# Another placement of the small pieces over the 44 iterations of a batch, and fewer filler matmuls in the last two units

## What is computed

```python
x = x + _L0_xattn_ref(_layernorm(x), ctx_512, ...)      # q,k,v and qc,kc,vc projections, two softmaxes, @ Wp
x = x + _L0_ffn_ref(_layernorm(x), ...)                 # gate, top-k tokens of each expert, two matmuls
# inside the first:
att = jnp.where(causal, einsum('bhqd,bhkd->bhqk', q, k) * scale, -inf)
y = einsum('bhqk,bhkd->bhqd', softmax(att), v) + einsum('bhqk,bhkd->bhqd', softmax(attc), vc)
```

## Time and profile before

| | |
|---|---|
| time, median of 3 runs | 1595.7 us (1590.92 to 1598.44) |
| the profiled execution: its time, its span | 1597.86 us, 1596.1 us |
| mean granted TensorE clock | 0.965 |
| busy in the span: PE, DVE, ACT, POOL | 95%, 70%, 57%, 34% |
| first exponential of batch 0, of batch 1, of batch 7; end of the last | 68.4, 216.9, 1111.3, 1249.8 us |

### The profile page before, as it was taken

How to read it: one execution, slowest core, us unless ns; L and a number is a source line. 1 busy time by engine, 2 the same in 40 slices (tenths; PEclk the granted TensorE clock), 3 DMA queues, 4 the chain that set the end, 5 groups by cost and what they waited for, 6 DMA issues and landing times. The chain is left out here.

```text
span 1596.1 us, 26481 instructions
## 1 busy us (share of the span) xinstructions
PE 1514.2 (95%) x9025; PEld 733.7 (46%) x9025; DVE 1123.7 (70%) x3056; ACT 910.7 (57%) x1754; POOL 546.1 (34%) x1009
## 2 busy tenths in 40 slices
PE   8899999999999999999999999999999868999997
PEld 4433444444444444444444444444443424666664
DVE  6878887887787788778877877788781274554441
ACT  2167777677766777677777677777767301112111
POOL 4122333442343225233433442451121302443342
PEclk9599999999999999999999999999999877999999
DMA  6776662855376556737672855377300211343432
GB/s 136 155 135 104 127 88 77 121 105 106 104 104 136 87 101 124 123 84 109 120 122 83 115 105 105 94 102 141 42 3 3 87 38 38 101 108 100 123 90 50
DMA packets 82490, 155.46 MB, mean 97 GB/s; under 512 B 13012, under 2 KB 46420, under 8 KB 82356
## 3 DMA queue, kind: packets, MB, share of 16 engines
q1 hardware_dynamic: 76212, 145.25, 47.0%
q0 software_dynamic: 6144, 8.52, 3.1%
HBM read 96.52 MB, written 53.08 MB: 94 GB/s over the span
## 5 line engine op out<-in xcount | busy, mean ns | idle before, releaser
L829 ACT ACTIVATE probs<-bank_ps 128x512 f32<-128x512 f32 (+1 forms) x1408 | 730.1, 579 | 247.9 <-PE bank_ps L613 239.0
L920 DVE TENSOR_REDUCE chunk_max<-bank_ps 128x1 f32<-128x512 f32 x1024 | 653.5, 683 | 144.0 <-PE bank_ps L652 140.2
L652 PE MATMUL bank_ps<-k_stack,q_stack 62*128 62x512 f32 (+3 forms) x1536 | 536.3, 432 | 7.4 <-DVE chunk_max L920 4.1
L613 PE MATMUL bank_ps<-q_stack,k_stack 64*128 64x512 f32 (+3 forms) x1536 | 512.8, 423 | 25.7 <-ACT probs L829 22.1
L652 PEld LDWEIGHTS bank_ps<-k_stack,q_stack 62*128 62x128 f32 x1536 | 248.2, 191 | 372.4 <-DVE chunk_max L920 202.2
L923 DVE CUSTOM_DVE_ANT_0 masked<-bank_ps,causal 128x128 bf16<-128x128 f32 (+3 forms) x512 | 232.9, 485 | 62.4 <-PE bank_ps L652 58.8
L631 PE MATMUL out_ps<-probs,v_cross 128*32 128x512 f32 x2048 | 275.7, 610 | 0.0
L613 PEld LDWEIGHTS bank_ps<-q_stack,k_stack 64*128 64x128 f32 x1536 | 234.5, 189 | 83.2 <-ACT probs L829 76.3
L1093 POOL TENSOR_TENSOR pool_idle<-pool_idle 128x1 f32<-128x1 f32 x292 | 56.4, 193 | 582.5 <-ACT probs L829 386.1
L1406 ACT ACTIVATE h<-h_ps,b1T 128x512 f32<-128x512 f32 x64 | 44.0, 687 | 254.5 <-PE h_ps L1352 220.4
L1352 PE MATMUL h_ps<-ff_yT,w1T 128*128 128x512 f32 x256 | 122.6, 615 | 1.0 <-DVE ff_yT L1419 1.0
(11 more groups left out here) (165 smaller groups left out, 1384.0 us busy)
## 6 DMA issues: line engine op xcount, KB each, us to landing
parts_dram<-parts SPq DMA_DIRECT2D x70, 512.0 KB, 2.7
k_stack<-parts_dram SPq DMA_DIRECT2D x180, 192.0 KB, 11.6
q_stack<-parts_dram SPq DMA_DIRECT2D x180, 128.0 KB, 10.5
w1T<-in_L_ffn_fc1s SPq DMA_DIRECT2D x8, 1024.0 KB, 5.0
w2T<-in_L_ffn_fc2s SPq DMA_DIRECT2D x8, 1024.0 KB, 7.3
z_rows<-z_sb SPq DMA_DIRECT2D x8, 528.0 KB, 3.1
x_sb<-in_x SPq DMA_DIRECT2D x8, 512.0 KB, 3.8
ctxT<-in_ctx SPq DMA_DIRECT2D x8, 512.0 KB, 4.1
```

Source lines behind the costliest of these rows:

```text
L613: mm = pe.matmul(bank_of(turn)[:, of.at:of.end], k_stack[base:base + SIDE, g, pair, of.keys:of.keys + P], q_stack[base:base + SIDE, g, pai ...
L652: return pe.matmul(bank[:, 0:n], q_stack[base:base + MAX_ROWS, g, pair, qc:qc + P], k_stack[base:base + MAX_ROWS, g, pair, k0:k0 + n], sta ...
L829: nc.scalar.activation(probs[:, buffer(u, i, p), side, columns], bank_of(("score", g, i, p, side))[:, columns], ACT.Exp, scale=SCALE)\
L920: nc.vector.tensor_reduce(dst, bank[:, 0:n], AX.X, ALU.max).then_inc(max_done, 1)
```

## The change

`PLAN` gets another placement of the same pieces. Iterations with no piece go from 9 to 15 of 44; iterations with two pieces go from 2 to 8, and four of these hold a large product beside another piece. The three tests on order that depend on the table follow it: `HALF_ORDER` (order in which a half's parts are stored), `EARLY` (how many of half 1 are stored ahead of `put_shift(3)`), and the place where PE waits for `y0T1`. In SP's list `put_shift(0)` now stands ahead of `fill(2)`. In the last batch a maximum without reader is issued only as the first and the last of an iteration: 38 of the 68 filler matmuls go. The output is the same.

```diff
 PLAN = {
-    (0, 1): (("out_cross", 0),), (0, 2): (("v", 1),), (0, 3): (("out_self", 0),), (0, 4): (("vc0", 1),),
...
+    (0, 2): (("vc0", 1),), (0, 3): (("out_cross", 0), ("out_self", 0)), (0, 4): (("v", 1),),
...
+EARLY = sum(half == 1 and name in HALF_PIECES and place < (2, 7) for place, names in PLAN.items() for name, half in names)
...
+HALF_ORDER = tuple(tuple(name for _, names in sorted(PLAN.items()) for name, half in names
+                         if name in HALF_PIECES and half == hf) for hf in range(2))
...
-                    project(("q", "qc", "k", "kc0", "kc1"), 0)
+                    project(HALF_ORDER[0], 0)
...
-                    project(("q",), 1)
+                    project(HALF_ORDER[1][:EARLY], 1)
                 put_shift(3, 4 * b + 3)
                 if not last:
-                    project(("qc", "k", "kc0", "kc1"), 1)
+                    project(HALF_ORDER[1][EARLY:], 1)
+                    put_shift(0, 4 * b + 4)
                     fill(2, 2 * b + 4, N_EXP * (4 * b + 3))
-                    put_shift(0, 4 * b + 4)
...
                         def maxima(n):
                             turn = ("max", g, i, n)
-                            bank_free(b, first, last, turn)
                             if used(turn, first, last):
                                 u, a = max_place(b, g, i, n)
+                                bank_free(b, first, last, turn)
                                 max_input(u // UNITS, u % UNITS, a, bank_of(turn)).then_inc(maxin_ready, 1)
-                            else:
+                            elif n in (0, A_AT[i] - 1):
+                                bank_free(b, first, last, turn)
                                 keep_array_busy(g, RING_TURNS.index(turn) % RING)
...
-                            if at[2:] == ("q", 0):
+                            if at[2:] in (("q", 0), ("qc", 0), ("k", 0)):
                                 pe.wait_ge(*freed(find_piece(b, first, last, "y0T1")))
```

More of the change, by code:

```diff
@@ L70 @@
 PLAN = {
[10 rows of a table removed]
[3 rows of a table added]
+    (1, 2): (("out_cross", 0),), (1, 3): (("k", 0),), (1, 5): (("out_self", 0),),
[3 rows of a table added]
+    (3, 6): (("out_self", 0), ("zT1", 0)), (3, 7): (("shift", 0),), (3, 8): (("gate", 0), ("vc1", 0)),
 }
@@ L359, in number_of @@
         def number_of(piece):
-            return 2 * len(HALF_PIECES) * piece.of + len(HALF_PIECES) * piece.half + HALF_PIECES.index(piece.name)
+            order = HALF_PIECES if piece.of == 0 else HALF_ORDER[piece.half]
+            return 2 * len(HALF_PIECES) * piece.of + len(HALF_PIECES) * piece.half + order.index(piece.name)
         def freed(piece):
@@ L451, in store_parts @@
                 sp.wait_ge(*halves_ready(piece))
-                if stacked and name == HALF_PIECES[0]:
+                if stacked and name == HALF_ORDER[hf][0]:
                     for slot in (2 * hf, 2 * hf + 1):
```

## The result

The changed kernel takes 1589.0 us, median of 10 runs (1581.4 to 1594.3); the kernel before, run beside it, 1596.5 (10 runs). The ratio is 0.995 [0.993, 0.9969]: about 0.5% faster, where 7 us slower was forecast. The profiled execution took 1589.25 us, its span is 1587.5 at a mean clock of 0.968.

What follows compares the result with a forecast made beforehand. PE was taken as the bound, busy 1142 of 1170 us in the attention, with only short waits to win. Full batches +7, SP's queue +3 and the last batch -3 gave +7 on 1595.7, so 1603 us; range 1590 to 1612.

Steps and rivals of the forecast that it cites:

- the second piece in an iteration therefore costs its whole length: Iterations with a large product: PE is the bound, nothing is given away, so a second piece adds its full length.
- a wait that did not "stay": At transpositions copied by ACT: waits of about 0.27 us each, as many after the change as before.
- the loss of a shift alone: Half behind the shift, (1, 7): 1.14 us against an estimated 0.9 without a wait, so 0.23 us given away.
- Empty iterations: Iterations without a piece: each gives away 0.37 us on PE; six more cost +2.2 us in a batch.
- the -0.5 at (3, 5): At (3, 5), where DVE is late with the maxima: longer iterations let it catch up, -0.5 us a batch.
- The wait for DVE that was allowed for in four empty iterations in a row: (1, 8) to (2, 0): 19 maxima in about 10.8 us, close to DVE's limit, costing 0 to +0.5 us.
- SP's queue: Start of unit 1: later shift read makes PE wait +0.5 us in each of batches 1 to 6, +3 together.
- Rival B: SP's queue late: batches 1 to 6 each wait 2 to 3 us at (1, 0); +19, 1613 us; chance 0.15.
- The last batch: Last batch: 38 fillers fewer bring -1.8 us, the table's moves there another -1; -3 us together.
- C: Batches' ends: with vc1 right behind gate the clock may not fall, -8.5 us, so 1594 us; chance 0.13.
- E: Last two units: clock falls because PE does less, up to 8 us, total +15, so 1611 us; chance 0.08.
- Rival D: The six new empty iterations give nothing away: sum -8 us, so 1587.5 us; chance 0.12.

Runs made afterwards that it cites:

- Run 3: Kernel before with proj0 moved from (1, 10) to (1, 7) behind the shift and out_cross from (1, 4) to (1, 5) beside out_self; 1590.9 us, one run.
- run 5: Changed kernel with all fillers back and vc1 moved from (3, 8), behind gate, to its own iteration (3, 9); 1587.2 us, ratio 0.9941.
- run 7: Kernel before with vc1 moved from (3, 6) to (3, 9), behind gate's product; 1600.3 us, ratio 1.0032.
- run 11: Changed kernel with zT1 beside the shift in (3, 7), zT0 with out_self in (3, 6), and (2, 10) emptied; 1588.6 us, ratio 0.9938.
- run 12: Kernel before with only zT0 moved from beside the shift in (3, 7) to (2, 9); 1589.6 us, ratio 0.9967.
- kernel 9: Kernel before with proj0 moved beside the shift in (1, 7), zT0 to (2, 9), and out_self and vc1 exchanged; 1580.3 us, ratio 0.9894.
- run 13: Kernel before with only out_self and vc1 exchanged, vc1 in (3, 5) and out_self in (3, 6); 1597.0 us, ratio 1.0011.
- run 8: The changed kernel once more, unchanged, in a later set; 1584.9 us, ratio 0.9941 to the kernel before.
- run 1: Changed kernel with all 68 fillers of the last two units put back; 1584.4 us, ratio 0.992 to the kernel before.
- Run 4: Changed kernel with the tokens' load ahead of put_shift(1) in SP's list instead of behind it; 1588.5 us, one run.
- Run 2: Kernel before, old placement, with the middle fillers left out; 1595.7 us, ratio 0.9994.
- run 6: New hand placement against the kernel before: a product beside each shift, 12 empty iterations, all fillers, old fill order on SP; 1583.0 us, ratio 0.9921.
- run 10: Hand placement of run 6 with out_self moved from the shift's iterations to the ones before, units 0, 2 and 3; 1582.9 us, ratio 0.9919.

## Why the prediction was wrong

**The full batch: +1.0 forecast, -1.1 measured.** This ledger prices each part as the iteration with it less an empty one with the same `i`, medians of batches 2 to 5, in us. The forecast column is what the prediction's prices give. The same piece differs by about 0.1 from place to place, so single entries are no better than that.

```
                                        forecast  measured
proj0, qc, v behind the shift              +0.78   -0.09   (-0.40, +0.06, +0.25)
oc+os, os+zT1, k+vc0, gate+vc1 as pairs    +1.48   +0.40   (+0.21, -0.03, -0.05, +0.27)
zT0 away from the shift                    -0.77   -0.59
out_self away from (3, 5)                  -0.50   -0.53
the other moves, the balance                0      -0.3
sum                                        +1.0    -1.1
```

**The step that failed is the sentence "the second piece in an iteration therefore costs its whole length"**, with "nothing is given away" beside a large product. By it each pairing costs the 0.37 of the iteration that it empties. Measured, the four pairs away from the shift cost 0.4 together instead of 1.5. The traces show where the 1.1 went. One part lies where two pieces meet, 0.6 in all. Four transpositions take 0.59 to the next matmul, eight directly behind one another only 1.02; in the single records the first comes 0.17 ahead of the second and the last 0.2 ahead of what follows, the others 0.11, and the pair has the longer steps once. This is (0, 3) of batch 4 after:

```profile
666.08 1.09 PE L669 MATMUL bank_ps<-ident,u_sb 128*128 128x128 f32 x8
667.11 0.38 PE L658 MATMUL bank_ps<-k_stack,q_stack 62*128 62x256 f32 x1
```

The lengths to the next maximum shrink by 0.16 for oc+os and for os+zT1, by 0.20 for k+vc0 (1.91 and 1.09 alone, 2.80 together) and by 0.09 for gate+vc1. Another 0.24 is a wait that did not "stay": behind zT1 alone the second half of the iteration took 0.91, behind the pair it takes 0.67. The rest is mostly the place of k+vc0, (3, 3), where an empty iteration gives away more than 0.37. Run 3 tests one pair by itself: 0.37 less 0.16 is its +0.21. Runs 5 and 7 give 0.26 and 0.27 for gate and vc1. The kernel before had such a pair already, in (0, 9), and its row could have warned me: 1.03 to the next maximum for two groups of transpositions.

```profile
695.57 1.09 PE L663 MATMUL bank_ps<-ident,x_sb 128*128 128x128 f32 x8
696.60 0.50 PE L652 MATMUL bank_ps<-k_stack,q_stack 62*128 62x512 f32 x1
```

**The second term that was wrong is the loss of a shift alone**, 0.23, from an estimate of three serial steps. A product takes the half from 1.14 down to 0.66, so 0.48 is won, and three times the difference is 0.7 to 0.8. The 0.18 that I put between the shift and a product in the scores' ring was right: 0.17 with qc, 0.16 with v. With proj0, which uses the other ring, there is nothing of it, and run 3 has the pair at -0.41 instead of +0.14.

*Empty iterations* give away what was forecast in most places: with the halves of other iterations of the same `i` beside them, 0.35 to 0.4. But they give away about 0.5 at i = 2 and 3, where the maxima of one half are narrower, and 0.25 at i = 10. The kernel before had three at i = 2 and 3, the changed kernel has none, so the six more come to +1.7 by this count, not to +2.2. In the ledger this is in the balance: out_cross costs 0.06 to 0.16 in its three places at i = 2 and 3, where it had cost 0.22.

*zT0* and *out_self* were right in sign and nearly in size (runs 11, 12 and 9). But the -0.5 at (3, 5) had another reason in the prediction, that DVE catches up in longer iterations. What did it is that out_self, which DVE must read, left the place where DVE is late: in kernel 9 the iterations around it stay as short as they were, vc1 stands in (3, 5), and the 0.5 is there. That this gain hangs on zT0's, the prediction didn't see (run 13). The wait for DVE that was allowed for in four empty iterations in a row didn't come: (1, 8) to (2, 0) take 10.6 us.

Over seven batches the full-batch error is about 15 us, as much as the whole miss (1603 forecast, 1589.0 measured); the errors below and the clock go both ways and nearly cancel.

**SP's queue: +3 forecast**, and fair as a mean, 2.4: over batches 1 to 6 the time lost at the start of unit 1 is 0.4 us in the first profile, 1.7 in run 8's, 1.9 in run 1's, 3.7 in run 5's and 4.5 in run 11's, all with the changed order on SP (the last two hold a stretch of half clock each). But it isn't +0.5 in each batch. Batch 1 has none, a batch from 2 to 5 at most 1.1 and mostly none; 10 of the 12 us fall on batch 6, and why there isn't shown. In batches 2 to 5 of these five profiles the context lands at T + 33.5 to T + 35.7 (forecast T + 35), in the first profile the read is issued 0.6 to 2.5 us ahead of the forecast in batches 2 to 6, and PE comes 0.4 us ahead of it. Run 4 shows where the wait for the read begins. Rival B, late in every batch, didn't occur, but its sign, kc0 waiting for the context, is in batch 6 of runs 5 and 11. (By its own terms, +19, its time should read 1615, not 1613.)

**The last batch: -3 forecast, +1** (139.6 in run 8 against 138.5). Run 2 gives 0.4 us for the fillers where I had 1.8, and that is within its noise: PE's waits for ACT at the scores grow from 3.7 to 6.3 us over the last two units. The moves that were to bring another -1 cost about as much instead; which of them, no run shows.

**The clock.** C's reason is refuted (run 7). But the clock is higher, 0.9717 against 0.9676 in one set, which by 0.83 us for 0.001 is 3.4 us of the gain there. A placement that touches neither shift nor (3, 5) stays at 0.968 (run 7); runs 5, 6, 9 and 10 lie at 0.972 to 0.973. Runs 12 and 13 didn't find the cause, and the kernel before itself lies between 0.967 and 0.969 from set to set. The profiles give a hint. Behind gate in batches 1 to 6, the five kernels that keep zT0 beside the shift in its old place (before, 2, 3, 7, 13) have 4, 3, 2, 3 and 3 stretches of half clock; the other ten executions, the changed kernel twice among them, have 0 to 2, 10 in all. Each is one execution, and nothing tests why it should be so: the cause stays open. E did not hold: the 17 us of half clock in the first profile's last batch are not in run 8's, with the same fillers left out.

**Rival D**, the only one near the measured time, hit the total by luck. Its reason was wrong: the empty iterations aren't free (1.28 from score to score); it is the pairings that cost far less than priced. The range ended at 1590, a microsecond above the first set's median; it was cut at C's weaker case, though no row that I used bounded what a second piece costs.

## What to carry to other kernels

Price a piece by the difference between iterations with it and without it, in each place where the trace has both, not by its length: the trace before had zT0 beside the shift (4.30 against 3.33) and out_self in (3, 5) (3.43 against 2.89), and repairing these two places and pairing proj0 with the shift beats the changed kernel's whole table by 5 to 9 us, part of which goes with the clock. Count each piece up to the next one, and look at a pair that the trace already has before pricing new pairs. When a move frees time on a busy helper engine, look at the next instruction that needs this helper: out_self's 0.7 us on DVE came back as a wait of 0.2 to 0.5 us one iteration later in three different placements (runs 6, 10, 13). And before a stretch of half clock in one profile is explained, look at the mean clock over all runs, since one profile had 17 us of it in the last batch and the next 3.4.

## What the runs showed of the hardware

- The run's time follows the mean granted clock almost linearly: 0.83 us for 0.001 over 79 runs of one kernel, correlation -0.94. The changed kernel's 1589.0 and 1584.9 in two sets come with 0.969 and 0.972; by that slope 2 of the 4 us are clock.
- Stretches at 1.2 GHz behind gate came in two of batches 1 to 6 in one execution of the changed kernel and in none in another, with the same instructions in each batch.
- Two groups of four transpositions take 1.03 us from the first to the next matmul when they stand directly behind one another, and twice 0.59 apart (kernel before and changed kernel).
- z_rows' store takes 13.7 us from issue to landing in the changed kernel, where it stands right behind a fill of 12 transfers, and 3.1 in the kernel before, where the fill began 23 us ahead of it (787.17 and 810.25 in the earlier trace rows). The pages' lists of transfers, before and after:

```profile
z_rows<-z_sb SPq DMA_DIRECT2D x8, 528.0 KB, 3.1
z_rows<-z_sb SPq DMA_DIRECT2D x8, 528.0 KB, 13.7
```
